# Three edits to where TensorE's filling work stands: output tiles of local attention in later chunks, latent values in the fourth chunk, first rows of the 64-expert layer tile by tile

## The reference

```python
x = _layernorm(x + rg_lru(x, ...))                 # stage A
x = _layernorm(x + experts_by_token_id(x, ...))    # stage B
x = _layernorm(x + moe64(x, ...))                  # stage C: 64 experts, top 4, capacity 64, 2 shared experts
x = _layernorm(x + sliding_window_attention(x))    # stage D: 32 heads of 16, window 128
x = _layernorm(x + fp8_quantised_product(x, ctx))  # stage E
x = _layernorm(x + latent_block(x, ...))           # stages F and G

# sliding_window_attention, for each block of 128 queries and its 256 keys
scores = where(valid, q @ k.T / sqrt(16), min);  out = softmax(scores) @ v;  return out @ Wo.T
# latent_block: attention over 16 heads of 32, from low-rank q_d and kv_d; half of each head's features are rotated (rope)
k_p, v = kv_d @ k_u_w, kv_d @ v_u_w;  k_r = rope(x @ rope_k_w);  q_p, q_r = q_d @ q_u_w, rope(q_d @ rope_q_w)
h = x + softmax(causal(q @ k.T / sqrt(32))) @ v @ o_w;  out = h + moe8(rmsnorm(h))
```

## Time and profile before

| what | value |
|---|---|
| median of 3 runs | 2498.3 us (2494.3 to 2504.02) |
| the profiled execution | 2500.3 us, its span 2498.3 us |
| TensorE busy (matmul) | 2247.5 us, 90% |
| VectorE, ScalarE, GpSimd busy | 1381.1, 657.9, 695.2 us |
| mean granted clock of TensorE | 0.956 |
| DMA | 235.40 MB, mean 94 GB/s |

### The profile page before, as it was taken

The page is one execution under the profiler, slowest core; times in us unless marked ns, Lnnn a source line. Parts: engine busy times, 40 slices in busy tenths (PEclk is TensorE's granted clock), DMA queues, the critical chain, the costliest instruction groups (busy, mean ns, idle before and its releaser), DMA issues. The chain is left out here.

```text
span 2498.3 us, 29517 instructions
## 1 busy us (share of the span) xinstructions
PE 2247.5 (90%) x10083; PEld 1030.3 (41%) x10086; DVE 1381.1 (55%) x3181; ACT 657.9 (26%) x1163; POOL 695.2 (28%) x1018
## 2 busy tenths in 40 slices
PE   9999997979999999898999997478888888799993
PEld 4444443435444443344444443233333333344441
DVE  6999883436412223555766774955656564422224
ACT  2222321212012121233434333433322322002223
POOL 2210002324523321133433333011113131125553
PEclk9999998999999999998999998689999999999997
DMA  8333102126047776163443330310000000064444
GB/s 293 117 101 112 40 4 72 64 76 243 10 133 247 236 234 202 40 165 83 90 85 78 84 71 2 109 71 1 2 18 2 18 27 18 17 199 83 87 88 149
DMA packets 101697, 235.40 MB, mean 94 GB/s; under 512 B 18919, under 2 KB 42647, under 8 KB 94399
## 3 DMA queue, kind: packets, MB, share of 16 engines
q1 hardware_dynamic: 79006, 191.83, 24.4%
q0 software_dynamic: 22560, 41.87, 7.7%
HBM read 174.69 MB, written 63.53 MB: 95 GB/s over the span
## 5 line engine op out<-in xcount | busy, mean ns | idle before, releaser
L1876 DVE CUSTOM_DVE_ANT_0 D_ps<-D_ps,D_mask 128x256 f32<-128x256 f32 (+1 forms) x512 | 186.9, 420 | 70.7 <-PE D_ps L1773 69.7
L1625 POOL TENSOR_SCALAR_AFFINE_SELECT D_probs<-D_probs 128x256 f32<-128x256 f32 x256 | 106.1, 420 | 286.7 <-ACT D_probs L1683 286.4
L1683 ACT ACTIVATE D_probs<-D_ps 128x512 f32<-128x512 f32 (+1 forms) x256 | 125.3, 543 | 165.0 <-PE D_ps L1795 164.8
L2876 DVE TENSOR_REDUCE F_neg_max<-F_ps 128x4 f32<-128x2048 f32 (+1 forms) x64 | 93.9, 1488 | 107.7 <-PE F_ps L2774 101.6
L3318 PE MATMUL G_ps<-G_gate_up,G_xgT 128*128 x304 | 138.5, 599 | 0.3 <-DVE G_xgT L3409 0.3
L2626 ACT ACTIVATE F_probs<-F_ps 128x1536 f32<-128x1536 f32 (+1 forms) x48 | 76.4, 1591 | 187.2 <-PE F_ps L2790 187.2
L1186 PE MATMUL C_ps<-C_down_shared,C_hs 128*128 128x512 f32 x256 | 114.0, 593 | 3.4 <-DVE C_hs L1353 2.3
L1174 PE MATMUL C_ps<-C_xT,C_gate_shared 128*128 128x512 f32 x256 | 115.4, 593 | 0.6 <-ACT C_xT L1049 0.6
L1174 PE MATMUL C_ps<-C_xT,C_up_shared 128*128 128x512 f32 x256 | 115.1, 592 | 0.0
L1773 PE MATMUL D_ps<-D_k_stack,D_q_stack 96*128 96x256 bf16 (+1 forms) x512 | 93.4, 268 | 8.8 <-DVE D_maxima L1876 7.2
L1023 POOL DMA_INDIRECT expert_sums<-C_y,C_of_slot x32 | 50.2, 1570 | 173.4 <-ACT C_y L1090 108.9
(11 more groups left out here) (496 smaller groups left out, 4531.1 us busy)
## 6 DMA issues: line engine op xcount, KB each, us to landing
C_ring<-moe_experts_dram SPq DMA_DIRECT2D x32, 1536.0 KB, 6.9
qk_parts<-D_parts SPq DMA_DIRECT2D x32, 384.0 KB, 2.5
B_w<-ctx_dram SPq DMA_DIRECT2D x8, 1024.0 KB, 6.0
expert_sums<-A_cq SPq DMA_DIRECT2D x1, 8192.0 KB, 29.4
C_ring<-expert_sums SPq DMA_DIRECT2D x5, 1536.0 KB, 10.4
D_q_stack<-qk_parts SPq DMA_DIRECT2D x16, 384.0 KB, 4.8
D_k_stack<-qk_parts SPq DMA_DIRECT2D x16, 384.0 KB, 7.7
B_w<-ctxT_dram SPq DMA_DIRECT2D x1, 4096.0 KB, 15.9
```

The lines of the kernel that those rows point to most:

```text
L1625: last = nc.gpsimd.affine_select(now[:, :, 0:P], now[:, :, 0:P], [[0, 2], [1, P]], ALU.is_ge, 0.0, base=0, channel_multiplier=-1)
L1683: nc.scalar.activation(probs[at % 2][:, 2 * pair:2 * pair + 2, 0:w], ps[:, 4 + unit % 3, :].rearrange("p (h q) -> p h q", h=2)[:, :, 0:w], ...
L1876: last = nc.vector.tensor_tensor_reduce(now, now, mask[:, first:256], 1.0, -3e38, ALU.add, ALU.max, maxima[n % 2][:, head, t:t + 1])
L2876: last = nc.vector.tensor_reduce(neg_max[n % 2][:, :, t], ps[:, 0:GROUP, at:at + w], AX_X, ALU.max, negate=True)
```

## The change

- Stage C: the first batch is loaded by four DMAs, one for each tile, with a semaphore each (`first_in`). `turn_first` turns tile by tile: it waits for a tile, transposes its four column blocks into PSUM banks 0 to 3, and signals a bank with the last tile. ScalarE copies from banks 0 to 3 for batch 0. The wait for the copy of two banks before begins at the third bank of batch 1. SP issues three DMAs more, all of them ahead of the constants.
- Stage D: output tiles 8 to 11 (batch 2) were made in chunk 12 (8 and 9, at places 10 to 15) and chunk 13 (10 and 11, at places 0 to 7). Now tile 8 is made in chunk 13, tiles 9 and 10 in chunk 14 and tile 11 in chunk 15, each from place 0 or 4 on. The rest of chunk 12 is spread anew: its key projection stands at places 8 to 11 (before: 7 to 9).
- Stage F: `values` of the next batch go from the third chunk (2, 6, 10) to the end of the fourth (3, 7, 11). The rule that puts the rest in place 8 no longer holds for fourth chunks (3, 7, 11, 15). With it the places change:

| chunk 2 | before | after |
|---|---|---|
| at 0, 1, 2 | rope4 rope5, rope5, rope5 | rope4, rope5, rope5 |
| at 4, 5, 6 | rope5 turn4, nope4 turn5, none | rope5, rope5, turn4 |
| at 7, 8 | nope5, values4 to 7 | none, nope4 turn5 nope5 |

| chunk 3 | before | after |
|---|---|---|
| at 0, 1 | rope6, rope7 | rope6, rope7 rope7 |
| at 4, 5 | rope7, rope7 | rope7 rope7, turn6 |
| at 7, 8, 9, 10 | none, rope7 turn6, none, none | values4, values5, values6, values7 |

Chunks 6 and 10 change as chunk 2 (their `turn` of the queries falls in place 5, and `count` follows the last nope), chunks 7 and 11 as chunk 3.

```diff
@@ -937,7 +937,7 @@
             return ring[tile // 3 % RING][:].rearrange("p e n -> p (e n)")[:, i * D:(i + 1) * D]
 
         consts_in, shared_in, down_in, cleared, slots_in = (sem(n) for n in ("consts_in", "shared_in", "down_in", "cleared", "slots_in"))
-        x_in, ring_in = sems("x_in", B), sems("ring_in", RING)
+        x_in, first_in, ring_in = sems("x_in", B), sems("first_in", GROUP), sems("ring_in", RING)
         empty_ready, converted = sem("empty_ready"), sem("converted")
         x_turned, xT_ready, logits_ready, max_ready, exp_ready, mask_ready, place_ready, placed, address_ready = (
             sem(n) for n in ("x_turned", "xT_ready", "logits_ready", "max_ready", "exp_ready", "mask_ready", "place_ready",
@@ -955,7 +955,8 @@
 
         @block.sync
         def _(sp):
-            sp.dma_start(acc[:, 0:4, :], x2[0:S, :].rearrange("(t p) n -> p t n", p=P)).then_inc(x_in[0], 16)
+            for t in range(GROUP):
+                sp.dma_start(acc[:, t, :], x2[t * P:(t + 1) * P, :]).then_inc(first_in[t], 16)
             for n, t in (("moe_router", router), ("moe_bias", bias), ("myself", myself)):
                 sp.dma_start(t[:], d[n]).then_inc(consts_in, 16)
             sp.dma_start(before32, d["before"]).then_inc(consts_in, 16)
@@ -1046,7 +1047,7 @@
             def keep_xT(b):
                 for k in range(KD):
                     act.wait_ge(x_turned, b * KD + k + 1)
-                    nc.scalar.copy(xT[:, k, b * S:(b + 1) * S], ps[:, 4 + k % 2, :]).then_inc(xT_ready, 1)
+                    nc.scalar.copy(xT[:, k, b * S:(b + 1) * S], ps[:, 4 + k % 2 if b else k, :]).then_inc(xT_ready, 1)
 
             def exponentials(b):
                 act.wait_ge(max_ready, b + 1)
@@ -1125,10 +1126,18 @@
 
         @block.tensor
         def _(pe):
+            def turn_first():
+                for t in range(GROUP):
+                    pe.wait_ge(first_in[t], 16)
+                    for k in range(KD):
+                        last = nc.tensor.transpose(ps[:, k, t * P:(t + 1) * P], acc[:, t, k * P:(k + 1) * P], ident[:])
+                        if t == GROUP - 1:
+                            last.then_inc(x_turned, 1)
+
             def turn_batch(b):
                 pe.wait_ge(x_in[b], 16)
                 for k in range(KD):
-                    if b * KD + k >= 2:
+                    if b * KD + k >= KD + 2:
 
                         pe.wait_ge(xT_ready, b * KD + k - 1)
                     for t in range(GROUP):
@@ -1229,7 +1238,7 @@
                                             ring[q % RING][:, e, KD * 2 * F_C:], start=True, stop=True)
                 last.then_inc(y_in_psum, 1)
 
-            turn_batch(0)
+            turn_first()
             pe.wait_ge(consts_in, 16 * 6)
             logits(0)
             turn_batch(1)
@@ -1478,6 +1487,7 @@
 
     FIRST, LAST, SLOTS = -3, CHUNKS + 1, 8
     MAXIMA = (3, 3, 3, 3, 2, 2, 0, 0)
+    LATE_OUTS = {CHUNKS - 4: (), CHUNKS - 3: (0,), CHUNKS - 2: (1, 2), CHUNKS - 1: (3,)}
 
     def jobs_of(i):
 
@@ -1493,7 +1503,9 @@
             jobs.append(("project", 2 * n + 1))
         if i % 4 >= 2 and (i + 2) // 4 < B:
             jobs += [("values", (i + 2) // 4 * 4 + i % 4 * 2 - 4 + t) for t in (0, 1)]
-        if i % 4 <= 1 and i >= 4:
+        if i in LATE_OUTS:
+            jobs += [("out", (B - 2) * 4 + t) for t in LATE_OUTS[i]]
+        elif i % 4 <= 1 and i >= 4:
             jobs += [("out", (i // 4 - 1) * 4 + i % 4 * 2 + t) for t in (0, 1)]
         return jobs
 
@@ -2313,7 +2325,7 @@
             return (front(b + 1) if ahead else gates(0, 0)) + (choice(b - 1) if b else [])
         if not ahead:
             return gates(0, 1) + [("count", b - 1)] if k == 2 else downs(0)
-        return features(b + 1, 0) + ([("count", b - 1)] if b else []) + values(b + 1) if k == 2 else features(b + 1, 1)[:3]
+        return features(b + 1, 0) + ([("count", b - 1)] if b else []) if k == 2 else features(b + 1, 1)[:3] + values(b + 1)
 
     def pieces_of(kind, n):
 
@@ -2337,7 +2349,7 @@
                 room = 0.0
                 while pieces and at >= (0 if pieces[0][:2] == ("gate", MF) else LAST_AT[pieces[0][0]]) + (pieces[0][1] % 4 if pieces[0][0] == "out" else pieces[0][1] % 2 * 2 if pieces[0][0] in ("gate", "up") else 0):
                     now.append(pieces.pop(0))
-            if i == -2 and at == 9 or at == 8 and (i == 0 or i > 0 and i % GROUP > 1):
+            if i == -2 and at == 9 or at == 8 and (i == 0 or i > 0 and i % GROUP == 2):
                 room = 1.0
             while pieces and (room >= 1.0 or at == 2 * SLOTS - 1 or spent + COST.get(pieces[0][0], 0.86) / 2 <= room * total):
                 spent += COST.get(pieces[0][0], 0.86)
```

## The result

The changed kernel takes 2512.7 us (median of 7 runs, 2511.7 to 2514.0), the kernel before 2494.3 on the same chip (2490.6 to 2506.5). On the 2498.3 us measured earlier for the kernel before, that is +14 us (+10.5 to +17.5), 0.56%: slower, clear of no change, with the half per cent inside the interval. The forecast was 2501.0 with a range of 2489 to 2510. The time, 2512.3 on that base, lies above the range; only the lower end of its interval, 2508.8, lies inside.

What follows compares the result with a forecast made beforehand. TensorE, busy 90% of the span, was taken as the bound. Local attention -0.4, 64-expert start -0.5 and latent attention +3.8 sum to +2.9 us, taking the median from 2498.3 to 2501; range 2489 to 2510.

Steps and rivals of the forecast that it cites:

- the price of a tile in T chunk 13: Local attention chunk 13: one output tile fewer, priced at 3.1 us a tile from chunks 13 against 14; -4 taken.
- T chunk 12: Local attention chunk 12: loses 8 pieces (-6.9 us), gets back 1.9 twice; -3.1, between -5 and -2.
- the bare chain: End of local chunk 12: without pieces, the chain from turned maxima to the next chunk's scores is uncovered; +1.9 us.
- SyncE's order: End of local chunk 12: the later key parts' write stands ahead of the three maxima DMAs; 0 to 2 us, 1.9 taken.
- Beside waits: Local chunk 15: 4 pieces in its first two slots, beside TensorE waits for the exponentials' cut; +1.2 us (0 to +3.4).
- Start: 64-expert layer's start: logits about 1.3 us earlier, but the second shared weight becomes the wait; -0.5 us (-1.3 to +1.5).
- the sum of -1.2: 64-expert layer's start: the skill's DMA fit (2.6 us for a 256 KB tile) would give -1.2 in place of -0.5.
- Latent, direct: Latent attention's third and fourth chunks: moved values cost +0.2 per fourth chunk, third chunks +0.5, clock +2.7; sum +3.8 us.
- I add 0.9 us a time: Latent chunks 2, 6, 10: low TensorE clock at the maxima scores after the wait for joined keys; 0 to 1.4 us.
- the serial chain: Nope, ScalarE, nope, ScalarE, join, scores bounds latent chunks 2, 6, 10 if scores come 1.5 us later; +14.6, 2513, chance 0.13.
- Nothing moves: Whole kernel: every gain is given back within its chunk; 2498 us, chance 0.22.
- TensorE's work alone: Whole kernel: every piece costs where it stood and is free where it goes; -22 us, 2476, chance 0.07.

Runs made afterwards that it cites:

- the kernel with the old places: Kernel before with only the local attention's outputs moved, chunk 12 keeping empty places so its key projection ends at place 9 as before; ratio 1.0023, +5.7 us.
- the start alone: Kernel before with only the 64-expert layer's new start (four tile loads, four transposes per tile); ratio 1.0008, +2.0 us.
- the values alone: Kernel before with only the latent values moved to the fourth chunks, place 8 rule edited; ratio 1.0012, +3.0 us.
- the outputs alone: Kernel before with only the local attention's output tiles spread over the late chunks; ratio 1.0038, +9.5 us.
- the combined kernel: Kernel before with values split two and two, one output tile moved from local chunk 13 to 15, four unread matmuls in its place; ratio 0.9967, -8.2 us.
- the split: Kernel before with the values' four pieces split, two at the third chunk's end and two in the fourth; ratio 0.9975, -6.2 us.

## Why the prediction was right and wrong

The sum was +2.9, it became +14. The step that failed is the price of a tile in T chunk 13; most of the other errors are clock that no term held. Point by point:

- **T chunk 12: -3.1 forecast, -2.9 measured** (29.98 to 27.06). Right, with its two reasons, the bare chain and SyncE's order, each forecast at 1.9. By the kernel with the old places (25.72) they are 2.6 and 1.3 inside the chunk, so the errors of the two cancel, and that the sum fits so well is luck. What failed is what was to follow. The forecast saw a DMA wait of over 1 us; it was 3.45, and it had booked no cost of the low clock behind it beyond a word in the next term.
- **T chunk 13: -4 forecast, +0.1 measured.** This is the step that failed. The "3.1 a tile", read as the difference between chunks 13 and 14, was taken as what comes back when a tile goes. VectorE's part is of that size while the clock stays high (3.7 us). But with the tile goes 3.4 us of TensorE work that kept the clock up; taking away one tile gave 1.3 us (28.12, clock 0.82). The other 1.4 (29.51 against 28.12) belong to the end of chunk 12: 0.4 goes with the queue's order (29.14 with the old places, wait 1.93), the remaining 1.0 with a chunk 12 whose end has no pieces; no run separates its clock from its waits.
- **T chunk 14: +5.5 forecast, +7.4 measured.** The tile price about holds when tiles are added: 29.07 with the old places, at a clock of 0.88, is 5.9 for two. The rest goes with the clock: 30.63 here, at 0.83, with the same work.
- **T chunk 15: +1.2 forecast, +3.0 measured**, 2.9 to 3.0 in four further kernels. "Beside waits" was wrong: the pieces stand in the first two slots, where the trace of the kernel before has one wait of 0.82 (the wait of 1.09 comes later), and at the low clock behind the wait for the maxima: the first two take 1.91 and 1.60 us, the next two 1.02 and 1.13.
- **Start: -0.5 forecast, about +1.2 measured** with the start alone (28.0 against the usual 26.8); inside the bounds, with the mechanism as told (wait for the second weight, 1.07 us). In the whole change the low clock in both logits hides it: 29.87, behind ScalarE and not the weight, so the sign "waiting for its weight" didn't show there. The base was mis-sized: 28.44 was an execution with a fall of the clock in it. The clock in the first logits, 1.6 to 2.0 us in all three executions with the new start, was in no term. And the sum of -1.2 that the prediction took from the fit in the Trainium skill doesn't follow from its own working: the tile's landing came out near the 2.6 us of that estimate, but where the weight ends the chain, 0.7 us at the rows' landing change nothing.
- **Latent, direct: +3.8 forecast, +2.2 measured** in the six chunks edited: 0.1 + 0.1, 0.2 + 0.2, 1.5 + 0.1. The fourth chunks at 0.13 to 0.16 and the new wait of 2.5 to 2.9 us with a low clock behind it are as told, but the scores took 1.23 us and not 2.09. In chunk 2 the 0.9 for the clock took the place of a wait of 0.95 that stood behind it, so it cost nothing there.
- **Latent, elsewhere: 0 forecast, +3.2 measured** (chunks 9 and 13 +1.6 each, 14 -1.65, the last projection +1.7). Another 0.9 is chunk 0 (31.53 against 30.67), which isn't the edit's: with the values alone it is 30.67; chunks 1 and 5 are 0.2 shorter. No step of the forecast had any of it. "I add 0.9 us a time" priced only what stands right behind a new gap. The bound of +8 for the latent part held it (6.1).

Of the rivals, the serial chain came nearest in time (2513) and not in place: it priced the L chunks at 9 and the clock of T chunks 13 and 14 at 5. Its point of decision wasn't reached: the scores stand 22.7 us after the start of chunk 2 (1763.02 - 1740.31), before at 23.2 (1754.40 - 1731.22), in chunk 10 1.0 later and not 1.5 (29.45 against 28.44), and chunks 2, 6 and 10 grew by 0.1, 0.2 and 1.5, not by 3. Its "+5 for a low clock" in the local attention is the part that was true, and it should have been in the sum. "Nothing moves" and "TensorE's work alone" fall with the outputs alone. The range ended 2.3 us too early because it left out most of this rival. The bounds as summed reach 2512.8 and would just have held the time, but by luck: chunk by chunk the local attention's bounds add up to +6.4, which the text narrowed to +5, and T chunks 13 and 14 and the local sum of +7.6 lie outside theirs.

What stays open: why the clock falls at one occurrence of the same two waits and not at another. The kernel before and the seven with its latent part have the same falls in their profiled executions though they start up to 10 us apart; the combined kernel has the split's latent part and other falls. No run here tells what decides it.

## What to carry to other kernels

Before you move filler work out of a chunk, ask what clock the rest of it will run at: in the chunks with waits of 1 to 2 us here, TensorE work was partly free or even less than free, and taking it away gave back a part of what its duration says (1.3 us of 3.4). Cover a serial chain with a part of the filler and spread the rest; moving all of it only moved the hole (2.90 us of wait; 0.55 with half of it left). And before pricing a change from one profile, look at whether the row you compare with was itself at a low clock.

## What the hardware showed that I had not expected

- Four added 128x512 matmuls made a chunk 2.45 us shorter (25.67 against 28.12), with TensorE's granted clock at 0.98 instead of 0.82 (26.33 and 0.94 in the combined kernel). Eight in the next chunk cost 0.9 us over two chunks instead of 6.9.
- Falls of the clock worth 1.6 us each came and went in chunks without any edit, with an edit whose nearest chunk ends over 30 us ahead of them, and repeated to 0.02 us between the two kernels that have the edit.
- SyncE's issue of three loads took 1.5 us or 11.4, depending on whether 4 MB of weights had been issued behind or before them.
